# Local attention: scores as three products of two fp32r parts, and a slot's values projected ahead of the first half of its scores

## What is computed

```python
qkv = shift_token(x) @ wqkv                      # 8 heads of 64
q, k = rotary_xpos(l2norm(q) * qs, l2norm(k) * ksc)
# windows of 128 queries; keys and values of the own and the last window
sim = einsum('bhwid,bhwjd->bhwij', 8.0 * q, k)   # then masked
o = einsum('bhwij,bhwjd->bhwid', softmax(sim), v)
x = x + o @ wo
```

## Time and profile before

| | |
|---|---|
| median of three runs | 1584.57 us |
| profiled execution: time, span | 1584.13 us, 1582.3 us |
| busy in the span: TensorE matmul, weight load | 1479.3 us (93%), 964.7 us (61%) |
| VectorE, ScalarE, GpSimd | 1037.2, 894.0, 521.1 us |
| L1624, scores, 512 instructions | 65.6 + 6.1 us busy |
| L1583, projections, 576 instructions | 150.4 us busy |
| local attention of layer 0 and of layer 1 | about 917 to 1139, 1255 to 1474 us |
| mean granted clock of TensorE | 0.985 |

### The profile page before, as it was taken

The page is one execution under the profiler, slowest core; times in us unless marked ns, Lnnn a source line. Parts: engine busy times, 40 slices in busy tenths (PEclk is TensorE's granted clock), DMA queues, the critical chain, the costliest instruction groups (busy, mean ns, idle before and its releaser), DMA issues. The chain is left out here.

```text
span 1582.3 us, 24385 instructions
## 1 busy us (share of the span) xinstructions
PE 1479.3 (93%) x9004; PEld 964.7 (61%) x9004; DVE 1037.2 (66%) x1879; ACT 894.0 (56%) x1852; POOL 521.1 (33%) x317
## 2 busy tenths in 40 slices
PE   8889999999987899999998889999999889999998
PEld 3432222222225679797987557777777667777776
DVE  3768888888818646465566545566597666666685
ACT  5137777777771343434252268778543488778341
POOL 7100000000004300000004277977433478877222
PEclk9999999999999999999999999999999999999999
DMA  7730222200000312030304120000100100000010
GB/s 245 157 41 12 31 41 41 41 2 1 1 12 14 123 53 69 14 107 13 107 7 137 40 70 2 1 1 2 61 20 0 57 2 1 1 1 28 5 50 27
DMA packets 59476, 64.84 MB, mean 41 GB/s; under 512 B 15154, under 2 KB 48706, under 8 KB 59380
## 3 DMA queue, kind: packets, MB, share of 16 engines
q1 hardware_dynamic: 58020, 60.17, 14.7%
q10 hardware_dynamic: 1360, 3.41, 0.6%
HBM read 52.88 MB, written 10.49 MB: 40 GB/s over the span
## 5 line engine op out<-in xcount | busy, mean ns | idle before, releaser
L581 DVE TENSOR_REDUCE mcol<-bank 128x1 f32<-128x1024 f32 x256 | 302.1, 1217 | 56.7 <-PE bank L572 56.7
L669 ACT ACTIVATE a_pt<-bank 128x512 f32<-128x512 f32 x512 | 266.5, 604 | 89.1 <-PE bank L701 89.1
L701 PE MATMUL bank<-qa,ka 99*128 99x512 bf16 x512 | 193.7, 386 | 7.6 <-ACT a_pt L669 3.8
L572 PE MATMUL bank<-ka,qa 96*128 96x512 bf16 x512 | 192.7, 384 | 4.5 <-DVE mcol L581 1.4
L2040 DVE CUSTOM_DVE_ANT_0 w_sm<-bank,mask 128x256 f32<-128x256 f32 (+1 forms) x256 | 88.9, 404 | 119.6 <-PE bank L1624 119.6
L1583 PE MATMUL bank<-wqkv,w_hst 128*128 128x512 f32 x576 | 150.4, 405 | 5.6 <-DVE w_sinp L1980 5.2
L701 PEld LDWEIGHTS bank<-qa,ka 99*128 99x128 bf16 x512 | 49.1, 98 | 165.7 <-ACT a_pt L669 121.3
L712 PE MATMUL bank<-a_pt,vst 128*32 128x512 f32 x1024 | 136.4, 605 | 0.1
L1875 ACT ACTIVATE w_sm<-w_sm,w_st 128x256 f32<-128x256 f32 (+1 forms) x256 | 123.9, 488 | 19.9 <-DVE w_st L2040 19.7
L1483 POOL TENSOR_TENSOR w_sm<-w_sm,w_st 128x1024 f32<-128x1024 f32 (+1 forms) x64 | 116.7, 1823 | 25.7 <-DVE w_st L2047 25.6
L1583 PEld LDWEIGHTS bank<-wqkv,w_hst 128*128 128x128 f32 x576 | 104.2, 189 | 28.9 <-issue 8.1
(11 more groups left out here) (254 smaller groups left out, 2842.1 us busy)
## 6 DMA issues: line engine op xcount, KB each, us to landing
f_wex<-in_W SPq DMA_DIRECT2D x8, 2048.0 KB, 12.0
qa<-q_parts SPq DMA_DIRECT2D x48, 128.0 KB, 4.3
ka<-k_parts SPq DMA_DIRECT2D x48, 128.0 KB, 5.0
q_parts<-p_parts SPq DMA_DIRECT2D x16, 192.0 KB, 3.3
k_parts<-p_parts SPq DMA_DIRECT2D x8, 384.0 KB, 3.5
wqkv_raw<-in_wqkv SPq DMA_DIRECT2D x2, 1536.0 KB, 6.8
w_raw<-in_w SPq DMA_DIRECT2D x2, 1408.0 KB, 5.9
phi<-in_phi SPq DMA_DIRECT2D x5, 512.0 KB, 3.9
```

The costliest lines, as they stand in the source:

```text
L572: last = nc.tensor.matmul(max_bank(G, r)[:, jh * HALF:(jh + 1) * HALF], G["qa"][k][0:KS, hg % 2, h, it * P:(it + 1) * P], G["ka"][k][0:KS, ...
L581: nc.vector.reduce_max(G["mcol"][hg % 2][:, p:p + 1], max_bank(G, r)[:, :], X).then_inc(G["max_free"], 1)
L669: nc.scalar.activation(pt[n % 2][:, q, :], sbank(HG * step + q), ACT.Exp, scale=HD0 ** -0.5).then_inc(p_ready, 1)
L701: mm(sbank(i), ka[k][:, q, n * P:(n + 1) * P], qa[k][:, ih, q, :], start=True, stop=True).then_inc(st_ps, 1)
```

## The change

The operands of the scores are no longer one fp32 tile each but two fp32r tiles. ScalarE's copies out of PSUM write part 0, and a new step on VectorE, `low_rows`, subtracts part 0 from the PSUM bank and writes part 1. A score half is 12 fp32r matmuls in place of 4 fp32 ones. The tile of the queries is no longer double-buffered, so its writers wait for the scores of the window before. On TensorE, `values` of a slot (with two waits of slots 13 and 15) stands ahead of `scores` half 0. On VectorE, `low_rows` stands ahead of `maxima` half 0, and `split_tokens` goes from the start of an odd slot to its end, behind `maxima` half 1.

```diff
-            kT = own("w_kT", [P, HP, 2 * WIN])
-            qT = own("w_qT", [P, 2, HP, P])
+            qTs = [own(f"w_qT_{c}", [P, HP, P], F32R) for c in range(2)]
+            kTs = [own(f"w_kT_{c}", [P, HP, 2 * WIN], F32R) for c in range(2)]
...
+        def place_of(i):
+            return slice(i % 2 * WIN, (i % 2 + 1) * WIN)
...
                 def scores(l, i, half):
                     if half == 0:
-                        pe.wait_ge(qT_done, (NG * l + i) + 1)
-                        pe.wait_ge(kT_done, (NG * l + i) + 1)
+                        pe.wait_ge(q_low, (NG * l + i) + 1)
+                        pe.wait_ge(k_low, (NG * l + i) + 1)
                     pe.wait_ge(s_masked, H1 * (NG * l + i) + 4 * half)
                     n = keys(i).stop
                     for p in range(2 * half, 2 * half + 2):
-                        for e in range(2):
-                            c0 = (p % 2) * 2 * WIN
-                            rows = slice(HD1 * e, HD1 * e + HD1)
-                            last = mm(S_PS[e][:, c0:c0 + n], qT[rows, i % 2, p, :], kT[rows, p, 0:n], start=True, stop=True)
+                        c0 = (p % 2) * 2 * WIN
+                        for c, (cq, ck) in enumerate(PRODUCTS):
+                            for e in range(2):
+                                rows = slice(HD1 * e, HD1 * e + HD1)
+                                last = mm(S_PS[e][:, c0:c0 + n], qTs[cq][rows, p, :], kTs[ck][rows, p, 0:n],
+                                          start=(c == 0), stop=(c == len(PRODUCTS) - 1))
                     last.then_inc(s_ps, 1)
...
                         if there(t):
                             queries_keys(l, t)
+                        if t == NG - 3:
+                            pe.wait_ge(xc_done, KD * (UNITS * l + 1))
+                        if t == NG - 1:
+                            pe.wait_ge(sd_done, UNITS * l + 1)
+                        if there(t):
+                            values(l, t)
                         if there(t - 2) and not (l and t == first):
                             scores(l, t - 2, 0)
...
                         if there(t - 4):
                             mixed(t - 4)
-                        if t == NG - 3:
-                            pe.wait_ge(xc_done, KD * (UNITS * l + 1))
-                        if t == NG - 1:
-                            pe.wait_ge(sd_done, UNITS * l + 1)
-                        if there(t):
-                            values(l, t)
                         if there(t - 3):
                             prob_rows(t - 3, 2)
...
                     def query_rows(i):
                         act.wait_ge(tq_ps, before(i) + 1)
-                        S(qT[:, i % 2, :, :], four(T_PS[0]), ACT.Copy).then_inc(qT_done, 1)
+                        act.wait_ge(s_ps, 2 * before(i))
+                        S(qTs[0][:, :, :], four(T_PS[0]), ACT.Copy).then_inc(qT_done, 1)
...
+                    def low_rows(i):
+                        dve.wait_ge(qT_done, before(i) + 1)
+                        dve.wait_ge(s_ps, 2 * before(i))
+                        V.tensor_tensor(qTs[1][:, :, :], four(T_PS[0]), qTs[0][:, :, :].bitcast(F32), ALU.subtract).then_inc(q_low, 1)
+                        dve.wait_ge(kT_done, before(i) + 1)
+                        V.tensor_tensor(kTs[1][:, :, place_of(i)], four(T_PS[1]), kTs[0][:, :, place_of(i)].bitcast(F32),
+                                        ALU.subtract).then_inc(k_low, 1)
...
                     for t in SLOTS1[first:]:
-                        if t % 2 == 1 and t < NG - 1:
-                            split_tokens(l, (t + 1) // 2)
                         if there(t - 3):
                             inverse_sums(t - 3, 1)
+                        if there(t - 2):
+                            low_rows(t - 2)
...
                         if there(t - 2):
                             inverse_sums(t - 2, 0)
                             maxima(t - 2, 1)
+                        if t % 2 == 1 and t < NG - 1:
+                            split_tokens(l, (t + 1) // 2)
```

More of the change, by code:

```diff
@@ L1331, in stage_layers @@
             "h_high", "h_low", "qk_ps", "v_ps", "qk_sb", "v_sb", "sq_done", "ss_done", "n_square", "n_sqrt", "rn_done"))
+        q_low, k_low = sem("w_q_low"), sem("w_k_low")
         (cos_done, sin_done, add_done, turn_done, tq_ps, tk_ps, qT_done, kT_done, s_ps, s_masked, e_done,
@@ L1855, in query_rows @@
                         act.wait_ge(tq_ps, before(i) + 1)
-                        S(qT[:, i % 2, :, :], four(T_PS[0]), ACT.Copy).then_inc(qT_done, 1)
+                        act.wait_ge(s_ps, 2 * before(i))
+                        S(qTs[0][:, :, :], four(T_PS[0]), ACT.Copy).then_inc(qT_done, 1)
                     def key_rows(i):
                         act.wait_ge(tk_ps, before(i) + 1)
-                        S(kT[:, :, (i % 2) * WIN:(i % 2 + 1) * WIN], four(T_PS[1]), ACT.Copy).then_inc(kT_done, 1)
+                        S(kTs[0][:, :, place_of(i)], four(T_PS[1]), ACT.Copy).then_inc(kT_done, 1)
                     def outputs(i):
```

## The result

The change makes the kernel slower. The median of the executions goes from 1584.65 to 1651.36 us, a ratio of 1.043 (95% interval 1.041 to 1.045). The forecast was 1638, with a range of 1604 to 1668. The profiled execution of the changed kernel took 1649.85 us with a span of 1648.1.

The account below looks back on a forecast made before the run. VectorE's chain from first maxima to probability copy, then TensorE's work in a row, was taken to bound each slot. Layer 0's 20.6, layer 1's 22.1 and the clock's 11.2 make 53.9; 1584.1 + 53.9 = 1638 us, range 1604 to 1668.

Parts of the forecast that it names:

- Values: TensorE: values' product ahead of the scores adds 1.40 us a slot, +16.8 per layer for t=4 to 15; slots 2, 3 +1.7.
- Late split: Odd slots' end: the token split, held beside GpSimd, stalls TensorE's next projection about 1.4 us, six times, +8.7 per layer.
- Score products: TensorE scores: 12 fp32r matmuls take 0.91 us a half instead of 1.06, 28 full-width halves, -4.3 us per layer.
- rival (c): TensorE scores: pairs of 64-row fp32r matmuls don't overlap, each half takes 1.64 instead of 0.91, 1679 us; chance 0.08.
- Subtractions free in steady slots: VectorE: query/key subtractions cost nothing in steady slots; exposed at t=16 and 17, 0.8 us each, +1.6 per layer.
- the junction: Start of layer 1: scores of slot 2 wait for two subtractions and hold back the projection, about +2.2 us once.
- The 0.5 for t=15: Slot 15: the values carry the wait for ScalarE's deviation forward, past its table load, +0.5 us per layer (0 to 1).
- Given back: At t=9 and t=11, TensorE's delays from a late GpSimd go as slots get longer, -4.4 us per layer.
- Clock: TensorE: longer idle in every slot lets the granted clock fall, 8 times at 1.4 us, +11.2 us in all.
- rival (d): TensorE: the clock falls in most slots, 25 us more than taken, 1663 us; chance 0.07.
- Rival (a): Whole slot: TensorE's work is the bound, so values cost the same anywhere and the change is faster, 1572 us; chance 0.07.
- rival (b): Odd slots' end: the token split causes no stall, 17.4 us less and fewer half-clock stretches, 1616 us; chance 0.20.

Follow-up runs that it names:

- the copy alone: The kernel before, with VectorE's copy of the probabilities put ahead of squared norms and sines: 1582.09 us, 0.9995 of before.
- GpSimd's exchange: The kernel before, with VectorE's probability copy ahead of squared norms and sines and GpSimd scaling window t-1 before turning window t: 1574.44 us, 0.9953.

## Why the prediction was right

**Values, 16.8 + 1.7 a layer: held.** Even slots take 14.50 us (982.83 to 997.33), odd ones 16.34, against a forecast of 14.5 and 16.1. The idle ahead of transposes 2 is 1.70 and 1.91 us, put down to the copy, as forecast. Moving the values alone costs 36.7 us on the kernel before, and 46.0 is their price together with the rest of the change; the prediction's terms for them were 16.8 + 1.7 in layer 0 and 16.8 + 1.0 in layer 1, some 36, with what the clock costs and what is given back booked in other terms. At t=3 the idle ahead of transposes 2 is 3.87 us where it was 2.63. The doubled output product shows that it is cover and not work that was lost.

**Late split, 8.7 a layer: held.** 12 stalls and 19.1 us against 17.4, with the subtraction at 2.27 us beside GpSimd as in the earlier trace rows. Taking the move back gave 22.4. Where the cast was caught as well the stall went beyond the forecast (1.66 us at t=5 of layer 0, 1.63 at t=13 of layer 1), most at t=3, here of layer 0:

```profile
944.25 1.22 PE L1587 MATMUL bank<-wqkv,w_hst 128*128 128x512 f32 x2 [2.63 <-DVE w_hst L1977]
...
939.98 1.91 DVE L1975 CAST w_hst<-xr 128x512 fp32r<-128x512 f32 x1
```

**Score products, -0.15 a half: held.** 0.91 us a group, as forecast; the pairs of 64 rows overlap, and rival (c) falls. The exact hit is partly luck: the fixed part read as 0.13 was rounded up to 0.2 with no row behind it, and the overlap was read from fp32 matmuls beside an fp32r group. (28 x 0.15 is 4.2 a layer, not the 4.3 of the sum, and six stalls of 1.4 are 8.4, not 8.7; this moves nothing.) The estimate of 1.28 us that the Trainium skill gives for twelve loads in a row (TensorE: Matmul & The Clock Gate, section LDWEIGHTS (loading the stationary operand)) is not what this case's trace shows for half rows: 0.91 us, and the measurement decides. The kernel without subtractions gained 14.2 us where 56 x 0.15 = 8.4 was forecast; its waits for the scores are about the same. Its executions show a granted clock of 0.985 to 0.987 against 0.982 to 0.984 for the kernel before beside them, some 10 us less at half clock, which at the prediction's 1.4 us for 3.4 is an estimated 4 of the other 5.8 us.

**Subtractions free in steady slots, 1.6 + 0.5 a layer and 2.2 at the junction: the steady slots and the junction held, the 1.6 by luck.** No steady slot's scores wait for them. All waits of the scores grew from 6.3 to 11.7 us, which is the predicted 1.6 + 1.6 + 2.2 = 5.4. But the parts are others. At t=16 the subtractions stand behind reciprocals that slot 15 left on VectorE, and the scores wait 3.17 us, where 1.84 was the wait before:

```profile
1137.62 0.98 PE L1629 MATMUL bank<-w_kT,w_qT 64*128 64x256 f32 x12 [3.17 <-DVE w_qT L2054]
...
1132.95 3.36 DVE L2032 RECIPROCAL n_xsum<-n_sqsum 128x256 f32<-128x256 f32 x2
1136.26 0.66 DVE L2054 TENSOR_TENSOR w_qT<-bank,w_qT 128x512 fp32r<-128x512 f32 x1
```

That is 1.33 us more instead of 0.8. At t=17 the wait grew from 0.79 to 1.62, as forecast, and at t=3 a wait of 0.54 for ScalarE went away, which the forecast had booked with the values. The three make 1.6 a layer. At the junction the wait is 2.08 against a predicted 2.2. The 0.5 for t=15 isn't seen: the projections of that slot start at 1119.17 with no idle time ahead.

More important, "free in steady slots" holds only in this company. With values and split in their old places four steady slots wait for the subtractions, and the scores' waits are 23.8 us in all. The cost of 26.6 us there is about the sum of three things: 17.3 us more waiting of the scores (23.8 against 6.5), half-clock time of 80 against 47 us, an estimated 14 us at the prediction's 1.4 for 3.4, and 5.2 us less waiting for the copy (11.6 against 16.8). The prediction read the cover from a slot of the old order and added that the moved values give more of it; it did not say what the split's place does to it. The split stands ahead of subtractions in VectorE's queue in both places. At the end of an odd slot, however, the next slot's projection waits for the same split, starts after it and so covers the subtractions: with the values back and the split late, no steady slot's scores wait (the 14.8 us are t=3, 16, 17 and the junction). At the start of an odd slot the projection runs during the split and is over too soon. So the change's parts don't simply add up: scores alone cost 14.5 and values alone 36.7, and the late split 22.4 where it was taken back.

**Given back, -4.4 a layer: held in part.** The clipping of 2 us at t=9 is gone in both layers, with the longer idle time and the half-clock stretch behind it; all 16 take 181 to 182 ns, where the earlier trace rows has one of 1.99 us (instances, then least, median and longest in ns):

```profile
L1996 DVE TENSOR_SCALAR w_nsq<-w_ss x16: 181/181/182, 906.8 to 1499.9; 128x32 f32<-128x32 f32 x16
```

The wait of 1.2 us for GpSimd at t=11 did not go away: it is 1.38 now, once in each layer. With the 2.4 us of the forecast off the 3.6 of before, 1.2 would be left; the trace has 2.8, so 1.6 us too much was taken as given back.

**Clock, +11.2: the mis-sized term.** The mean granted clock fell from 0.985 to 0.972. At half clock a stretch counts for half, so the time at 1.2 GHz is (1 - 0.985) x 2 x 1582 = 47 us before and (1 - 0.972) x 2 x 1648 = 92 us after. From 915 us to the end of the second attention the kernel before has 4 stretches of the 3.4 us in the earlier trace rows, the changed one 16. The two at t=9, which the forecast had booked as given back, are gone, so 14 are new, where 8 were taken. At the prediction's 1.4 us a stretch the 6 others are 8.4 us, the larger part of the 13 us between 1638 and 1651. Of the rest, 1.6 is the wait above and 1.7 the split's stalls (19.1 against 17.4). The last 2 us were not located.

The stretches also fell in other places than the prediction reasoned from. It took them from the idle of 1.7 to 1.9 us in every slot, but of the 24 steady slots only 5 have one. Of the others seven lie around slots 2 and 3 of the layers (one before), where TensorE stands for up to 3.87 us at a time, two follow the wait of 2.08 us at the junction (none before), and two the waits of 3.17 us at t=16 (one before). They begin (three times one runs straight on into a second) inside a wait of TensorE or within 1.4 us after its end. The one at t=3 of layer 0, as length, busy time of each engine, granted clock, share of DMA and GB/s:

```profile
933.90:940.70 6.80, 4.81 (x34) 3.96 (x35) 4.77 (x16) 5.67 (x14) 5.16 (x3) 0.50 0.00 0
```

So rival (d), a fall in most slots, went too far: 26 stretches were its price, and most steady slots have none.

Rival (a), TensorE as the bound, is refuted by the doubled product, rival (b), no stall, by the 12 waits at line 1587. TensorE's busy share of 90% after the change would still suggest (a).

What stays open is which state of the array, idle time or kind of matmul, makes the clock fall. Half-clock time was about 47 us before, 80 with only the scores changed ((1 - 0.975) x 2 x 1595.7), 54 with fp32 products in the same schedule (0.983, 1598.0 us), and 47 again with fp32r products and no subtractions (0.985, 1570.3 us). The four executions of each agree with this order: 0.975 to 0.979, 0.978 to 0.983, 0.985 to 0.987; the kernel before has 0.982 to 0.986, so that 54 can't be told from 47. Neither fp32r matmuls nor waits for the subtractions do it alone.

## What to carry to other kernels

In a pipelined slot, the place of a step on a busy engine can be worth more than the step: find for every idle gap which other engine's chain ends it, and treat the work that fills the gap as cover; here six matmuls a slot moved out of it cost 37 us with no instruction added, and 41 us of work put into the gap cost nothing. Before an operation is called free because its engine waits, look at what stands ahead of it in the queue in every slot, also in the few disturbed ones, and at whether another engine's running instruction can hold that up. And when a chain is cut, look for the next one from the same event: the copy alone gave nothing that can be measured, with GpSimd's exchange it gave 0.5%. A disturbed slot costs twice: TensorE's long waits, not the short idle time of every slot, are where most of the half-clock stretches stood.

## What was not expected of the hardware

- Two VectorE steps that read only SBUF were held until a running GpSimd instruction ended, a cast and a subtraction: the cast 1.91 and 2.03 us where its median before the change is 0.42, and the subtraction 3.59 us where it took 0.69 alone. Two in a row were both caught (2.03 + 3.59 us in the kernel with only the scores changed). The subtraction of the same width that reads a PSUM bank and one SBUF tile took 0.65 to 0.69 us in all 64 instances after the change. By the Trainium skill (SBUF — State Buffer, section Who interferes with whom) a VectorE instruction with two SBUF inputs contends with a GpSimd instruction that reads SBUF, one in a mode that uses both ports contends with GpSimd too, and one with at most one SBUF input outside those modes doesn't. The trace agrees on both kinds of subtraction. For the cast, with its one SBUF input, it agrees if the cast ran in such a mode, which no row shows. That two steps in a row can be caught, and for 5.6 us, only the rows show.
- A held subtraction ended 0.55 us after GpSimd's instruction in both timelines above (1008.69 and 1009.24; 1010.64 and 1011.19), close to its 0.69 us alone.
- 12 fp32r matmuls of 64 rows and 256 columns in two row halves took 0.91 us to the next group, 0.15 less than 4 fp32 ones of the same shape.
- Filling idle times of 1.7 us with work lowered the half-clock time from 92 to 82 us ((1 - 0.975) x 2 x 1644.8) and the time by 4.7 us (ratios 1.0377 to 1.0412 against 1.0408 to 1.0452, which just touch): redundant work was at least no loss.
